# Selective state-space block on one core: the state between chunks on 128 rows of 128 columns, in place of 16 rows of 1024

## The reference

```python
xr, gate = jnp.split(x @ W_in.T, 2, axis=-1)
xr = xr + t_emb[:, None, :]
xc = silu(depthwise_causal_conv4(xr, W_conv) + b_conv)
xn = layernorm(xc) * ln_g + ln_b
Bm, Cm, dt = jnp.split(xn @ W_xproj.T, 3, axis=-1)
dt = jnp.tanh(dt @ W_dt.T + b_dt) * 0.01
Ad = 1.0 + dt * -jnp.tanh(A_log)
Bd = Bm * jnp.minimum(norm(xn), 1.0)
def step(h, inputs):
    ad, bd, xt, ct = inputs
    h = jnp.clip(h * ad[:, :, None] + bd[:, :, None] * xt[:, None, :], -10.0, 10.0)
    return h, jnp.einsum('bd,bdh->bh', ct, h)
y = scan(step) + D * xn
out = x + y * silu(gate) @ W_out.T
```

## Time and profile before

| | |
|---|---|
| median of 3 runs | 2100.95 us (2098.36 to 2104.25) |
| the profiled execution's own time | 2097.88 us |
| its span, first to last instruction | 2095.8 us |
| PE busy | 1936.1 us (92%) |
| POOL busy | 1801.3 us (86%) |
| DVE busy | 1641.5 us (78%) |
| ACT busy | 1439.5 us (69%) |

### The profile page before, as it was taken

The page is one execution under the profiler, slowest core; times in us unless marked ns, Lnnn a source line. Parts: engine busy times, 40 slices in busy tenths (PEclk is TensorE's granted clock), DMA queues, the critical chain, the costliest instruction groups (busy, mean ns, idle before and its releaser), DMA issues.

```text
span 2095.8 us, 46902 instructions
## 1 busy us (share of the span) xinstructions
PE 1936.1 (92%) x16784; PEld 1466.0 (70%) x16784; DVE 1641.5 (78%) x2075; ACT 1439.5 (69%) x3494; POOL 1801.3 (86%) x1444
## 2 busy tenths in 40 slices
PE   5589999999999999999999999999999999999988
PEld 5467777777777777777677777777777777777765
DVE  3377887888877887878887888887888877888786
ACT  4677667777667777767777767677766777766753
POOL 1389988889988989898889998898998888998887
...
DMA packets 83016, 120.16 MB, mean 57 GB/s; under 512 B 22352, under 2 KB 51408, under 8 KB 78112
## 3 DMA queue, kind: packets, MB, share of 16 engines
...
## 4 chain that ended last, share of the span: by engine, by line
PE 64%; issue 11%; ACT 11%; DVE 10%; SPq 2%; POOL 1%; DMA 1%; DVEq 0%; ACTq 0%; POOLq 0%
PE ps_y L574 13%; PE ps_job L492 8%; PE ps_fill L547 7%; PE ps_job L455 7%; PE ps_fill L538 7%; PE ps_job L468 5%; PE ps_job L450 4%; DVE ks L984 3%; PE ps_y L554 3%; PE ps_y L560 3%; PE ps_job L462 3%; DVE h L931 2%; PE ps_job L478 2%; ACT xh L668 2%; ACT low L778 2%
## 5 line engine op out<-in xcount | busy, mean ns | idle before, releaser
L1082 POOL TENSOR_TENSOR prod<-ks,crep 128x512 f32<-128x512 f32 x1024 | 1289.2, 1279 | 187.8 <-PE ps_y L574 175.7
L984 DVE TENSOR_TENSOR_SCAN ks<-low,ps_fill 128x512 f32<-128x512 f32 x1024 | 1216.9, 1208 | 266.9 <-PE ps_fill L547 257.4
L778 ACT COPY low<-ps_fill 128x512 f32<-128x512 f32 x1024 | 590.1, 580 | 489.0 <-PE ps_fill L538 485.9
L574 PE MATMUL ps_y<-c_sb,prod 128*128 128x128 f32 x4096 | 613.5, 275 | 2.9 <-POOL prod L1082 1.4
L574 PEld LDWEIGHTS ps_y<-c_sb,prod 128*128 128x128 f32 x4096 | 464.3, 142 | 81.5 <-issue 45.0
L538 PEld LDWEIGHTS ps_fill<-ts,xs 128*128 128x128 f16 x4096 | 317.1, 99 | 172.3 <-issue 11.9
L538 PE MATMUL ps_fill<-ts,xs 128*128 128x128 f16 x4096 | 399.2, 220 | 11.7 <-DMA xs<-h 7.2
L547 PE MATMUL ps_fill<-spans,pick 128*128 128x512 f16 x1024 | 392.2, 383 | 6.8 <-ACT low L778 6.6
L450 PE MATMUL ps_job<-x,w_in 128*128 128x128 f16 x3072 | 226.8, 228 | 46.1 <-ACT xr L730 37.3
L737 ACT ACTIVATE tap<-xr,cols_sb 128x128 f32<-128x128 f32 x768 | 251.4, 391 | 16.3 <-PE ps_job L468 16.2
L450 PEld LDWEIGHTS ps_job<-x,w_in 128*128 128x128 f16 x3072 | 197.4, 103 | 59.6 <-issue 58.3
...
## 6 DMA issues: line engine op xcount, KB each, us to landing
...
xs<-xh SPq DMA_DIRECT2D x256, 64.0 KB, 2.7
xs<-xl SPq DMA_DIRECT2D x224, 64.0 KB, 2.0
...
ts<-tth SPq DMA_DIRECT2D x128, 32.0 KB
ts<-tth SPq DMA_DIRECT2D x128, 31.0 KB
```

The source lines that it names most:

```text
L574: last = mm(ps_y[:, cut], prod[:, s % HOLD, e, :], ident, start=False, stop=(u % 4 == 3 and q == 3 and e == QN - 1), is_transpose=True)
L778: copy(low[:, (TILES * k + s) % RING], ps_fill[:, (TILES * k + s) % RING]).then_inc(sem["low_copied"], 1)
L984: nc.vector.tensor_tensor_scan(ks[:, u % 2, QN * q:QN * (q + 1)].rearrange("d n t -> d (n t)"), low[:, g % RING], ps_fill[:, g % RING], 0. ...
L1082: tt(prod[:, i % HOLD], ks[:, u % 2, part], crep[:, p, part], ALU.mult).then_inc(sem["weighed"], 1)
```

## The change

The state lies on 128 rows: row `8 n + e` holds block `e` (128 channels) of state `n`.
- `kend` is laid out by state and then block, and one transpose of 128x128 replaces eight of 128x16. VectorE takes it in one instruction. `lend`, which comes out of `carry` on 16 rows, is spread to 128 rows by a transfer.
- The two factors of the first step (B's first column and the decay) lie in `bd` on 16 rows. A new job `bd` (point 19, bank 1) multiplies them by a 16x128 table of zeros and ones (`spread`), which repeats each on 8 rows. VectorE then copies them out and does the whole step at point 20: multiply, multiply-add, clip. ACT's L704 is gone.
- `x0` is written to DRAM and read back onto the 128 rows; it has its own memory.
- `h16` is 128x128. ACT's cast moves from point 41 to 25, GpSimd's subtract from tile 21 to 16.
- `nb` moves from point 25 to 26, both `carry` and `out` by one; `xr`'s first half is taken at 22 in place of 23, `bc` made at 19 in place of 20, the bounds at 23 in place of 22. The taps are made 1 to 3 points earlier, with four buffers in place of three. `prod` has six buffers in place of four.

```diff
-HOLD = 4
-TAPRING = 3
+HOLD = 6
+TAPRING = 4
...
-        h1 = sb("h1", [NS, DI])
-        lend = sb("lend", [NS, 2, DI])
+        h1 = sb("h1", [P, P])
+        x0 = sb("x0", [P, P])
+        lend = sb("lend", [NS, DI])
+        lend128 = sb("lend128", [P, 2, P])
...
-        h16 = sb("h16", [NS, 2, DI], H)
-        x0 = h16[:].rearrange("n h d -> n (h d)").bitcast(F)
+        h16 = sb("h16", [P, 2, P], H)
...
-        TAP_AT = [26, 31, 33, 36, 39, 42, 45, 49]
+        TAP_AT = [24, 28, 30, 34, 38, 40, 43, 46]
...
-                    sp.dma_start(x0, xn[0:1, pn].rearrange("o (n d) -> o n d", n=1).broadcast_to([1, NS, DI])).then_inc(sem[f"x0_in{pn}"], 16)
+                    since(sp, "x0_in", 16 * j)
+                    sp.dma_start(x0_dram, xn[0:1, pn]).then_inc(sem["x0_out"], 16)
                     for jj in range(NSUB):
...
+                    sp.wait_ge(sem["x0_out"], 16 * (j + 1))
+                    since(sp, "bd_taken", j)
+                    sp.dma_start(x0[:], x0_dram.broadcast_to([NS, DI])).then_inc(sem["x0_in"], 16)
                     sp.wait_ge(sem["xl_done"], j + 1)
...
+                    sp.wait_ge(sem["lend_set"], 2 * j + 2)
+                    if exists(k, -1):
+                        sp.wait_ge(sem["hend_taken"], k)
+                    sp.dma_start(lend128[:, pn], lend[:]).then_inc(sem[f"lend_in{pn}"], 16)
                     sp.wait_ge(sem["carry_taken"], 2 * j + 2)
...
-                    for e in range(4):
-                        last = tr(ps[0:NS, e * P:(e + 1) * P], kend[:, q, 4 * i + e, :], ident)
+                    last = tr(ps[:, 0:P], kend[:, q].rearrange("d n e -> d (n e)"), ident)
+                elif name == "bd":
+                    last = mm(ps[:, 0:2], spread, bd[:], start=True, stop=True)
...
+                elif name == "bd":
+                    pe.wait_ge(sem["bd0_set"], j + 1)
+                    pe.wait_ge(sem["decay0"], j + 1)
...
+                    copy(bd[:, 0:1], bank("zT")[0:NS, 0:1]).then_inc(sem["bd0_set"], 1)
...
-                    act_fn(first_decay[:], ad[:, 0, 0:1], ACT.Identity, scale=p_end[:, 1 - p:2 - p]
+                    act_fn(bd[:, 1:2], ad[:, 0, 0:1], ACT.Identity, scale=p_end[:, 1 - p:2 - p]
                            ).then_inc(sem["decay0"], 1)
-                for i in at("h0", 1):
...
-                    act_fn(bank("h0", i)[0:NS], x0[:, i * BANK:(i + 1) * BANK], ACT.Identity, scale=zT[:, 0, 0:1]
-                           ).then_inc(sem["h0_ready"], 1)
...
+                    stt(h1[:], lend128[:, 1 - p], -1.0, bank("hend")[:, 0:P], ALU.mult, ALU.add
+                        ).then_inc(sem["hend_taken"], 1)
...
+                if point == TAKE["bd", 0] and exists(k, 1):
+                    u = bank("bd")[:, P:2 * P]
+                    dve.wait_ge(sem["bd_ready"], j + 1)
+                    dve.wait_ge(sem["x0_in"], 16 * (j + 1))
+                    nc.vector.tensor_copy(bd128[:], bank("bd")[:, 0:2]).then_inc(sem["bd_copied"], 1)
+                    dve.wait_ge(sem["bd_copied"], j + 1)
+                    tsc(u, x0[:], bd128[:, 0:1], None, ALU.mult).then_inc(sem["u0_set"], 1)
+                    dve.wait_ge(sem["u0_set"], j + 1)
                     if first_chunk(j):
...
+                        stt(u, h1[:], bd128[:, 1:2], u, ALU.mult, ALU.add).then_inc(sem["u1_set"], 1)
+                        dve.wait_ge(sem["u1_set"], j + 1 - BATCH)
+                    tsc(h1[:], u, CLIP, -CLIP, ALU.min, ALU.max).then_inc(sem["bd_taken"], 1)
...
-                tt(prod[:, i % HOLD], ks[:, u % 2, part], crep[:, p, part], ALU.mult).then_inc(sem["weighed"], 1)
+                tt(prod[:, g % HOLD], ks[:, u % 2, part], crep[:, p, part], ALU.mult).then_inc(sem["weighed"], 1)
```

More of the change, by code:

```diff
@@ L413, in _ @@
             for c in range(DB):
[L414 removed]
+                last = mm(ps_fill[:, 2, c * NS:(c + 1) * NS], lend[:, c * P:(c + 1) * P], small[:, 0:NS],
                           start=True, stop=True)
@@ L573, in flip @@
                 for e in range(QN):
-                    last = mm(ps_y[:, cut], prod[:, s % HOLD, e, :], ident, start=False,
+                    last = mm(ps_y[:, cut], prod[:, (TILES * k + s) % HOLD, e, :], ident, start=False,
                               stop=(u % 4 == 3 and q == 3 and e == QN - 1), is_transpose=True)
@@ L754, in side @@
                     copy(ch[:, half], bank("carry", i)).then_inc(sem["carry16"], 1)
-                    since(act, "hend_taken", 2 * k)
-                    copy(lend[:, 1 - p, half], bank("carry", i)[0:NS]).then_inc(sem["lend_set"], 1)
+                    if exists(k, 0):
+                        act.wait_ge(sem[f"lend_in{p}"], 16 * pair(k, p, 0))
+                    copy(lend[:, half], bank("carry", i)[0:NS]).then_inc(sem["lend_set"], 1)
                 if point == 27 and exists(k, 1):
@@ L880, in side @@
                         ).then_inc(sem["z_taken"], 1)
-                for i in range(2):
-                    if point != TAKE["hend", i] or not exists(k, -1):
-                        continue
-                    half = slice(i * BANK, (i + 1) * BANK)
-                    dve.wait_ge(sem["hend_ready"], 2 * (k - 1) + i + 1)
-                    dve.wait_ge(sem["lend_set"], 2 * k)
+                if point == TAKE["hend", 0] and exists(k, -1):
+                    dve.wait_ge(sem["hend_ready"], k)
+                    dve.wait_ge(sem[f"lend_in{1 - p}"], 16 * pair(k, p, -1))
                     if exists(k, 0):
```

86 lines of the change are left out of this document (31 added, 55 removed), and 3 rows, old and new, of the table JOBS.

## The result

The changed kernel takes 2082.4 us (2082.2 to 2086.27, 4 runs), the kernel before 2099.65 (2098.04 to 2104.25, 4 runs): a ratio of 0.9919, 95% interval 0.9898 to 0.9939. It is faster, by 17 us, but not by the 80 that I predicted, and 14 us outside my range. The profiled execution took 2086.27 us.

The account below looks back on a forecast made before the run. TensorE, 92% busy, was taken as the bound, its idle time mainly waits for ACT's `xr` and VectorE's `h`. Terms summed to -80.1 us, giving 2020.9 us on the median of runs, stated as 2020, range 1990 to 2068.

Parts of the forecast that it names:

- The two waits: TensorE's waits at L450 for ACT's `xr` and at L475 for VectorE's `h` both go: -37.3 and -37.2 us.
- ACT's order: ACT's copies from tile 16 on make TensorE's widening of tile 19 wait 0 to 0.8 us a chunk: +12.4 us.
- `HOLD`, `TAPRING` and the moved taps cost nothing by themselves: Six `prod` buffers (`HOLD`), four tap buffers (`TAPRING`) and the earlier tap points were priced at nothing.
- The transposes and `bd`: On TensorE, one end transpose replaces eight, -14.1 us; the new product `bd` takes 0.25 us a chunk, +8.0 us.
- The start: Once, ahead of the loop, `x0` lands some 6 us later: +3 us, bounds 0 to 6.
- The rings at nothing: The larger buffer rings, six for `prod` and four for taps, were claimed to cost nothing.
- My slack for GpSimd: GpSimd's products are ready 1.5 us before TensorE's flip, 0.5 without the two new `prod` buffers; cost nothing.
- The clock: Nine drops to 1.2 GHz, 1.65 us each, go with the pair of TensorE gaps: -14.9 us, other end 0.
- The queue: DMA: `x0` through DRAM lands 4.5 us after issue, `h` 3.1 us after with 1.4 us slack; cost nothing.
- (b): Rival: the chunk's end waits for `h`, loaded in 256 B runs; +54 us, time 2073 us; chance 0.07.
- (d): Rival: `x0` lands late and VectorE's block holds up scans that TensorE's fills need; 2107 us and up; chance 0.05.
- (a): Rival: TensorE loses 1.3 us a chunk at tiles 15 to 19 to ACT or GpSimd; about 2062 us; chance 0.14.

Follow-up runs that it names:

- E3: Changed kernel with taps and the points of `nb`, `carry` and `out` all as before; new layout and larger rings stay: 2016.24 us, ratio 0.9608.
- E12: Kernel before, with only ACT's copy of `xr` moved ahead of the bounds: 2103.18 us, ratio 1.0023.
- E8: Changed kernel with `bc` back at point 20, behind the four state instructions: 2054.8 us, ratio 0.9792.
- E5: Changed kernel with only `nb` (and its take) back from point 26 to 25: 2052.94 us, ratio 0.9782.
- E14: E9 with `nb` alone moved late, from point 25 to 26: 2005.58 us, ratio 0.9556.
- E10: E1 with `bc` at point 20 (old taps, late points): 2054.31 us, ratio 0.9787.
- E13: E9 with `carry` (31, 36) and `out` (41) alone moved late: 2053.46 us, ratio 0.9782.
- E15: E9 with the changed kernel's new tap points alone: 2043.58 us, ratio 0.9736.
- E9: E3 with `bc` moved from point 19 to 20; the fastest version found: 2005.57 us, ratio 0.9555.
- E17: E13 with ACT's `carry` copies ahead of the taps where they share a point (31 and 36): 2033.69 us, ratio 0.969.
- E18: E15 with ACT's copies of the first `carry` ahead of the taps of point 30: 2022.75 us, ratio 0.9638.
- E1: Changed kernel with the taps at their old points, four tap buffers kept: 2091.47 us, ratio 0.9961.
- E6: Changed kernel with only `carry` (30, 35) and `out` (40) back at their old points: 2089.61 us, ratio 0.9958.
- E16: E9 with three tap buffers in place of four: 2006.06 us, ratio 0.9558.
- E11: E3 with four `prod` buffers in place of six: 2031.07 us, ratio 0.9677.
- E4: Changed kernel with four `prod` buffers in place of six: 2099.92 us, ratio 1.0002.

## Why the prediction was wrong, step by step

*The two waits* (-37.3, -37.2): both are gone in the changed kernel, as forecast. In E3, with `nb` at its old point, 0.39 us a chunk are still there: VectorE is not as early as I worked out. And I summed the two as if each had a price of its own. E12 shows that VectorE's `h` set both; only a change that frees VectorE earns either. This one does, so the sum took no harm from it.

*The step that failed: "ACT's order. Here I expect a loss ... So it waits 0 to 0.8. I take 0.4: +12.4."* Place, mechanism and sign were right; the size was not. TensorE waits 0.39 + 1.10 us for the copies, and further on 0.28 + 0.42 (0.63 + 0.42 one time in eight) that I had not followed at all: 69 us in all, in place of 12.4. With that the sum is -80.1 - 12.4 + 69 = -23.5 against 2097.88, so 2074.4; the profiled execution took 2086.27. The 12 us between are about what TensorE's longer products cost, a term that my sum does not have: of 58.72 us a chunk the transposes and `bd` should have left 58.72 - 0.77 + 0.25 = 58.20, and 58.70 are there, 0.50 x 31 = 15.5 us. They go with the waits (58.10 in E3, where these are gone); why a product takes longer, no run shows. Three things made up the 69 us.
- "Or 0.8 later if its `bqm` must wait for VectorE": it waits 1.78 us, since VectorE is 1.6 us later than I had it (1.15 - 0.41 for the scan, 1.44 - 0.58 for `bc`). I had put both in at their lengths of before. E8 took 0.87 of this away and gained 27.6 us.
- `nb` one point later puts a third scan ahead of `nbh`. While VectorE is late this costs 29 us (E5), and nothing when it is in time (E14, and with the late carries E10 against E13, 0.9 us). I had moved TensorE's side only.
- "`HOLD`, `TAPRING` and the moved taps cost nothing by themselves" and "the second `carry` moves behind it": I counted ACT's load up to the copy of tile 19 and no further. The copies of `carry`, `xl` and `gated` come next: the taps cost 38 us alone (E15), the later carry and out 48 alone (E13). Together they cost no more than one, 49 (E8 and E10 against E9): all lengthen one chain, ACT's taps, carry copies, VectorE's `xl`, `gated`, TensorE. That chain is read from the traces; E17 and E18 test one link of it. It also fits that in the changed kernel undoing one part alone did not help: in E1 and in E6 alike a row of taps stays directly ahead of a carry's copies, and the longest wait of `xl` is 2.39 and 3.32 us, against 2.21.

*The transposes and `bd`* (-14.1, +8.0): L465's wait grew from 0.34 to 0.67 us, as worked out. `bd` takes 0.38 us, not 0.25: 4 us more, inside my bounds. Three of the four instructions of VectorE's block take more than the 281 ns that I gave as their bound (0.35, 0.36, 0.29), but the copy takes 0.12, and the block its 1.1 us.

*The start* (+3): the first `nb` comes at 66.2 us in place of 65.7, so 0.5.

*The rings at nothing*: half wrong. The tap buffer costs nothing in E9 (E16). The two `prod` buffers are worth 17 us in the changed kernel and 15 in E3. My slack for GpSimd held: TensorE does not wait for `prod`. What I missed is that GpSimd's phase sets the length of two VectorE instructions. In E11 that accounts for 10 of the 15 us. In E4 the scan of `pf` takes 1.55 us too, but the loss shows mostly as longer products of TensorE and at the end of the run; how it comes to that stays open.

*The clock* (-14.9): the nine drops went, 14.9 us by my price, and it is the only gain left. *The queue*: right; `x0` and `h` land sooner than I allowed, so rivals (b) and (d) are out in the changed kernel (in E9 the first wait for `h` shows).

*The rivals*: (a), "ACT or GpSimd takes the place of the waits", is what happened, at 2.2 us a chunk in place of its 1.3, longer products on top, and without its clock drops. It had 0.14. (Two of the rivals' times don't come out of their own terms: (a)'s 2020.9 + 29 + 15 is 2065, not 2062, and (b)'s 2020.9 + 54 is 2075, not 2073. Neither moves the range.) I gave the forecast 0.60 on a term that I bounded at 0.8 us by ACT's busy time, when the trace of before could have warned me: one of the 32 instances of `bc` there, the one that started just behind such an end, took 1.52 us.
